# Cross-attention kernel: scores by high parts of both banks first, and x's split ahead of exp and normalise

## The reference

```python
def _layernorm(x, axis=-1, eps=1e-05): ...
x = x + _L0_xattn_ref(ctx_1024, _layernorm(x), fside, fside, ...)   # layernorms with weights, q/k/v, softmax(q k^T), @ Wout
#   q = q * (1.0 + scale) + shift ;  qk = einsum(q, k) * 64**-0.5 ; attn = softmax(qk) ; out = attn @ v @ Wout
x = x + tanh(_layernorm(x) @ weight @ aux_weight1 @ aux_weight2 + bias)
```

## Time and profile before

| | |
|---|---|
| median of 3 runs | 2071.06 us (2065.18 to 2071.54) |
| profiled execution | 2069.4 us |
| its span | 2067.6 us |
| TensorE's mean granted clock | 0.997 |
| busy: PE, DVE, ACT, POOL | 98%, 76%, 66%, 67% of the span |
| DMA packets | 464.11 MB, SyncE's queue 79.2% of 16 engines' span |

### The profile page before, as it was taken

How to read it: one execution, slowest core, us unless ns; L and a number is a source line. 1 busy time by engine, 2 the same in 40 slices (tenths; PEclk the granted TensorE clock), 3 DMA queues, 4 the chain that set the end, 5 groups by cost and what they waited for, 6 DMA issues and landing times.

```text
span 2067.6 us, 31929 instructions
## 1 busy us (share of the span) xinstructions
PE 2017.8 (98%) x9072; PEld 1661.6 (80%) x9072; DVE 1573.8 (76%) x2470; ACT 1364.1 (66%) x3125; POOL 1393.7 (67%) x1529
## 2 busy tenths in 40 slices
PE   8998999999999999999999999999999999999998
PEld 6887878888788788878888788878888788878887
DVE  7567876776677787787777877778777877888776
ACT  4455667666676766776667676666666666666654
POOL 2136767666577777677766777777776777777664
PEclk9999999999999999999999999999999999999999
DMA  7657989989788788978898798888877567866663
GB/s 259 196 176 219 275 233 256 265 241 262 210 249 256 207 236 242 260 217 225 233 260 242 205 234 238 243 229 221 230 228 241 171 204 208 236 197 196 189 171 121
DMA packets 524864, 464.11 MB, mean 224 GB/s; under 512 B 56720, under 2 KB 416272, under 8 KB 524688
## 3 DMA queue, kind: packets, MB, share of 16 engines
q1 hardware_dynamic: 524688, 462.06, 79.2%
HBM read 279.64 MB, written 182.26 MB: 223 GB/s over the span
## 4 chain that ended last, share of the span: by engine, by line
PE 32%; DVE 18%; SPq 15%; ACT 10%; issue 10%; POOL 7%; DMA 4%; DVEq 0%; ACTq 0%; POOLq 0%
PE bank L168 12%; PE bank L1246 8%; PE bank L173 6%; POOL area L1547 5%; PE bank L1251 4%; DVE pT_lo L1430 3%; ACT area L1291 3%; DVE turned L1421 3%; DVE area L1399 2%; ACT pT_hi L1296 2%; DVE row_max L1404 2%; SPq L1127 2%; SPq L726 2%; SPq L1145 2%; SPq L1157 2%
## 5 line engine op out<-in xcount | busy, mean ns | idle before, releaser
L1547 POOL TENSOR_TENSOR area<-area,row_max 128x256 f32<-128x256 f32 x512 | 353.0, 710 | 105.3 <-DVE row_max L1404 100.1
L1296 ACT CAST pT_hi<-turned 128x512 fp32r<-128x512 f32 x256 | 159.3, 622 | 400.8 <-DVE turned L1421 400.7
L168 PE MATMUL bank<-M_hi,xT_hi 128*128 128x512 f32 x1024 | 402.7, 393 | 14.4 <-ACT xT_hi L1080 14.4
L168 PE MATMUL bank<-M_lo,xT_hi 128*128 128x512 f32 x1024 | 401.4, 392 | 0.0
L1571 POOL TENSOR_TENSOR area<-area 128x512 f32<-128x512 f32 x127 | 165.4, 1302 | 269.1 <-ACT area L1337 269.1
L1554 POOL TENSOR_TENSOR area<-area,row_inv 128x512 f32<-128x512 f32 x256 | 269.1, 1051 | 113.7 <-DVE row_inv L1413 113.7
L1410 DVE TENSOR_REDUCE row_sum<-area 128x8 f32<-128x512 f32 x256 | 174.5, 682 | 169.5 <-ACT area L1291 168.6
L1430 DVE TENSOR_TENSOR pT_lo<-turned,pT_hi 128x512 fp32r<-128x512 f32 x256 | 196.6, 768 | 112.3 <-ACT pT_hi L1296 103.7
L173 PE MATMUL bank<-M_hi,xT_lo 128*128 128x512 f32 x1024 | 276.0, 391 | 3.6 <-POOL xT_lo L1085 3.6
L1246 PE MATMUL bank<-N_hi,pT_hi 128*128 128x512 f32 x640 | 249.5, 390 | 3.2 <-ACT pT_hi L1296 1.8
L1246 PE MATMUL bank<-N_lo,pT_hi 128*128 128x512 f32 x640 | 249.6, 390 | 1.5 <-issue 1.4
(11 more groups left out here) (211 smaller groups left out, 4547.9 us busy)
## 6 DMA issues: line engine op xcount, KB each, us to landing
p_scratch<-area SPq DMA_DIRECT2D x256, 256.0 KB, 3.1
p_moved<-p_scratch SPq DMA_DIRECT2D x512, 128.0 KB, 4.2
area<-x_dram SPq DMA_DIRECT2D x128, 256.0 KB, 5.0
area<-x_turned_dram SPq DMA_DIRECT2D x128, 256.0 KB, 4.4
x_scratch<-area SPq DMA_DIRECT2D x127, 256.0 KB, 3.4
x_moved<-x_scratch SPq DMA_DIRECT2D x508, 64.0 KB, 3.5
y_dram<-area SPq DMA_DIRECT2D x127, 256.0 KB, 3.5
land<-m_scratch SPq DMA_DIRECT2D x120, 256.0 KB, 3.2
```

What stands on the lines that cost most here:

```text
L168: mm = eng.matmul(ps, sh, mv, start=(n == 0), stop=False)
L1296: act.copy(half_of(pT_hi, q), turned[:]).then_inc(s_pTh[q], 1)
L1547: last = pool.tensor_tensor(s, s, row.to_broadcast([P, 2, 4, J2]), ALU.subtract)
```

## The change

From tile 3 on the scores are made in another order (`scores_high_first_pe`): for bank 0 and then bank 1 the eight matmuls with `xT_hi`, then for bank 0 and bank 1 the four with `xT_lo`. Each bank's semaphore is raised by its last matmul. ScalarE splits the next tile's x ahead of exp of bank 0 (from slot 3 on), GpSimd ahead of its two `normalise`. In a border slot ScalarE evacuates both banks of the N2 step, and VectorE makes all eight low parts; the second semaphore that GpSimd's part needed is gone. Slots 0 to 2 stay as they were.

```diff
--- before.py
+++ after.py
@@ -603,7 +603,7 @@
         s_n, s_nh, s_nl = sem("s_n"), sem("s_nh"), sem("s_nl")
         s_bin = sem("s_bin")
         s_x2a, s_x2n = sem("s_x2a"), sem("s_x2n")
-        s_last, s_nfree, s_nl_pool = sem("s_last"), sem("s_nfree"), sem("s_nl_pool")
+        s_last, s_nfree = sem("s_last"), sem("s_nfree")
         s_yl, s_bnl, s_rsl = sem("s_yl"), sem("s_bnl"), sem("s_rsl")
         s_kh, s_kl = sem("s_kh"), sem("s_kl")
         s_wo2, s_nev = sem("s_wo2"), sem("s_nev")
@@ -696,9 +696,6 @@
             used, free = free[1], (used, free[0])
         N_of = lambda b: [n_bufs[i] for i in n_at[b]]
         stage_of = lambda b, c: n_raw[:, (n_at[b][1] * PAIRS + c) * D:(n_at[b][1] * PAIRS + c + 1) * D]
-        BY_POOL = (4, 5, 6)
-        BY_DVE = {0: [c for c in range(PAIRS) if c not in BY_POOL], 1: list(range(PAIRS))}
-        lo_before = lambda b: PAIRS * min(b, STACKED) + sum(len(BY_DVE[a % 2]) for a in range(STACKED, b))
         split_at = {TPB * b + c - TPB + 2: (b, c) for b in range(STACKED + 1, B, 2) for c in range(PAIRS)}
         border = lambda t: t % TPB == 1 and t // TPB in range(STACKED, B, 2)
         n2_ps = banks[2:4]
@@ -778,14 +775,7 @@
             for c in cs:
                 eng.wait_ge(s_nh, PAIRS * b + c + 1)
                 hi, lo = (n_cols(y, c) for y in N_of(b))
-                eng.tensor_tensor(lo, stage_of(b, c), hi.bitcast(F32),
-                                  ALU.subtract).then_inc(s_nl if c in BY_DVE[b % 2] else s_nl_pool, 1)
-
-        def n2_made(pe, b, q):
-            of_half = range(4 * q, 4 * q + 4)
-            pe.wait_ge(s_nl, lo_before(b) + sum(c < 4 * q + 4 for c in BY_DVE[b % 2]))
-            if b % 2 == 0 and any(c in BY_POOL for c in of_half):
-                pe.wait_ge(s_nl_pool, len(BY_POOL) * ((b - STACKED) // 2) + sum(c < 4 * q + 4 for c in BY_POOL))
+                eng.tensor_tensor(lo, stage_of(b, c), hi.bitcast(F32), ALU.subtract).then_inc(s_nl, 1)
 
         m_where = lambda c: ((c // 2) % 4, 2 * (c // 8) + c % 2)
         in_pairs = lambda a: a.rearrange("p (i a j) -> p i a j", i=2, j=J2)
@@ -1108,6 +1098,26 @@
             at_least(pe, s_sb[q], t)
             passes(pe, S_ps[q][:], [(st(xT_hi, k), st(xT_lo, k), mo(M_hi_now, k), mo(M_lo_now, k)) for k in range(DC)],
                    (lambda: pe.wait_ge(s_xTl, t + 1)) if q == 0 else None).then_inc(s_sc[q], 1)
+
+        def scores_high_first_pe(pe, t, m):
+            M_hi_now, M_lo_now = M_hi[t // TPB % 2], M_lo[t // TPB % 2]
+            st = lambda y, k: y[:, k * P:(k + 1) * P]
+            mo = lambda y, k, q: y[:, k * INNER + q * BANK:k * INNER + (q + 1) * BANK]
+            pe.wait_ge(s_xTh, t + 1)
+            for q in range(2):
+                if m == 0:
+                    pe.wait_ge(s_ll, t - 4 + 4 * q)
+                elif m == 2 and t < TPB * STACKED:
+                    pe.wait_ge(s_nl, t + 3 + q)
+                pe.wait_ge(s_sb[q], t)
+                for k in range(DC):
+                    for i, mv in enumerate((M_hi_now, M_lo_now)):
+                        pe.matmul(S_ps[q][:], st(xT_hi, k), mo(mv, k, q), start=(k == 0 and i == 0), stop=False)
+            pe.wait_ge(s_xTl, t + 1)
+            for q in range(2):
+                for k in range(DC):
+                    mm = pe.matmul(S_ps[q][:], st(xT_lo, k), mo(M_hi_now, k, q), start=False, stop=(k == DC - 1))
+                mm.then_inc(s_sc[q], 1)
 
         def slot_sp(sp, t, m):
             def store(place, u=t):
@@ -1208,15 +1218,13 @@
                 if (t, place) in tile_at:
                     tile_pe(pe, tile_at[t, place])
 
-            if t < T:
+            if 2 < t < T:
+                scores_high_first_pe(pe, t, m)
+            elif t < T:
                 for q in range(2):
                     if t == 0:
                         pe.wait_ge(s_ml, 8 * q + 8)
                         pe.wait_ge(s_kbo, 15 + q)
-                    elif m == 0:
-                        pe.wait_ge(s_ll, t - 4 + 4 * q)
-                    elif m == 2 and 2 < t < TPB * STACKED:
-                        pe.wait_ge(s_nl, t + 3 + q)
                     scores_pe(pe, t, q)
             if t != 2:
                 tile("A")
@@ -1234,10 +1242,8 @@
                 at_least(pe, s_x2, u)
             for q in range(2):
                 if tile_of(t - 2):
-                    if m == 2 and u < TPB * STACKED:
+                    if m == 2:
                         pe.wait_ge(s_nl, u + 4 + 4 * q)
-                    elif m == 2:
-                        n2_made(pe, u // TPB, q)
                     hi, lo = N_of(u // TPB)
                     ks = range(4 * q, 4 * q + 4)
                     pe.wait_ge(s_pTh[q], u + 1)
@@ -1349,6 +1355,8 @@
                 xT_split_hi(act, t + 1)
             if t > 2:
                 evacuate("A")
+                if t < T - 1:
+                    xT_split_hi(act, t + 1)
             if t < T:
                 exp(0)
             if t < 2:
@@ -1365,12 +1373,13 @@
                 fold_n_act(act, 0, range(5, 6))
                 land_hi(act, 0)
                 fold_n_act(act, 0, range(6, 7))
-            elif t < T - 1:
+            elif t == 2:
                 xT_split_hi(act, t + 1)
-            if t == 2:
                 ln1_stats(act, 3, 3)
             if t in stacked_at:
                 n2_evacuate(act, act.copy, *stacked_at[t], 0)
+                if border(t):
+                    n2_evacuate(act, act.copy, *stacked_at[t], 1)
             evacuate("C")
             if border(t):
                 n2_hi(act, t // TPB, range(0, 4))
@@ -1511,7 +1520,8 @@
                 dve.tensor_tensor(xr[u % RING], O_ps[:], xr[u % RING], ALU.add).then_inc(s_x2, 1)
             sum_tile("C")
             if t in stacked_at:
-                n2_evacuate(dve, dve.tensor_copy, *stacked_at[t], 1)
+                if not border(t):
+                    n2_evacuate(dve, dve.tensor_copy, *stacked_at[t], 1)
             if tile_of(t - 1):
                 if t >= 4:
                     dve.wait_ge(s_x2Tl, t - 3)
@@ -1523,13 +1533,13 @@
                     maximum(0, 2)
                 turn_p(0, t - 1)
                 if border(t):
-                    n2_lo(dve, t // TPB, BY_DVE[0][0:2])
+                    n2_lo(dve, t // TPB, range(0, 2))
                 if t == 1:
                     read_scores(1, 2)
                     maximum(1, 2)
                 pT_lo_part(0, t - 1)
             if border(t):
-                n2_lo(dve, t // TPB, BY_DVE[0][2:])
+                n2_lo(dve, t // TPB, range(2, 8))
             if t in split_at:
                 b, c = split_at[t]
                 n2_lo(dve, b, [c])
@@ -1590,19 +1600,17 @@
             if t == 2:
                 land_lo(pool, 1)
                 xT_split_lo(pool, 3)
+            if 2 < t < T - 1:
+                xT_split_lo(pool, t + 1)
             if t < T:
                 normalise(0)
                 normalise(1)
             if t == 1:
                 land_lo(pool, 0)
-            if 2 < t < T - 1:
-                xT_split_lo(pool, t + 1)
             if 1 < t < T - 1:
                 pow1(pool, t + 1)
             if tile_of(t - 4) and t - 4 < LAST - 1:
                 pow2(t - 4)
-            if border(t):
-                n2_lo(pool, t // TPB, BY_POOL)
             if t == 5:
                 land_lo(pool, t)
 
```

## The result

The changed kernel takes **2082.95 us** (median of 4 runs, 2079.28 to 2084.91) against 2069.57 of the kernel before (four runs, the three of the table ahead among them): a ratio of 1.0069, 95% interval 1.0046 to 1.0091. That is 13.4 us slower. The forecast was 2071, "no difference"; the range (2050 to 2086) holds the result, the sign was missed. The profiled executions differ a little more: the spans are 2067.6 and 2083.1 us, 15.5 apart.

A forecast was written before the change was run, and what follows sets the result against it. TensorE is 98% busy, but a VectorE-to-VectorE loop of 13.77 us, within 0.6 us of TensorE's time, limits gains. Terms 0, +11.1, 0 and -9.2 make +1.9 on 2069.4: 2071 us, range 2050 to 2086.

The forecast's parts named there:

- xT_lo ahead of normalise: Slots 10 to 25: SyncE's second p store goes 0.79 us later per slot; 14 steps make +11.1 us.
- My upper bound, +15: Slots 10 to 25: loss if Wo's store takes 0.3 us more; lower bound 0 if M's store lands earlier.
- Slots 83 to the end: Sum of plain slots -6.5, two borders -2.0 and 14 N2 slots -0.7: -9.2 us.
- Contention: Plain slots: VectorE's pT_lo no longer beside GpSimd's xT_lo, -0.27 us each; 24 behind slot 83 make -6.5.
- The N2 slots: Behind slot 83: 14 slots at the loop's 14.45 us instead of TensorE's 14.50, -0.7.
- The borders: N's low parts and copies redistributed: -2.0 us at the last two borders, about +0.4 each at the four before.
- Slots 26 to 82: Late x about +2 and border +0.4, four times, against 1.9 given back by seven plain slots: 0, bounds -6, +9.
- x comes too late for exp: Rival, chance 0.20: ScalarE's xT_hi waits for its load before exp of bank 0, slots 27 to 81; +9, 2080 us.
- the waits simply go: Rival, chance 0.25: loops have slack, TensorE keeps 14.4 us of xT_hi and six times 0.75 of xT_lo; 2050 us.
- the port only changes hands: Rival, chance 0.13: GpSimd's small power takes xT_lo's place, pT_lo still waits, the 6.5 us aren't given back; 2077 us.
- Slots 4 to 9: Within slots 3 to 9, where TensorE sets the pace: 0.
- Score order: Bank 0 finished 1.8 us later, VectorE waits 0.1 to 0.3 us or keeps phase: cost 0; 0.3 a slot without cover.

The follow-up runs named there:

- the two edits that relieve this loop: Changed kernel with xT_lo behind normalise in slots 10 to 25: 0.9996; changed kernel with SyncE's M store behind the first p store, slots 4 to 25: 0.9957.
- the early store: Changed kernel with SyncE's store of the M tile moved, in slots 4 to 25, from slot's end to right behind the first store of p: 2059.9 us, 0.9957.
- The square above: Four kernels with score order and xT_hi moved; last two borders: neither further part 62.0 us, N part alone 60.4, xT_lo move alone 58.0, both 56.1.

## Why the prediction was wrong

**The step that failed** is the size of "xT_lo ahead of normalise". The mechanism was right in place and kind: the two edits that relieve this loop, each in another way, gave the loss back (0.9996 and 0.9957 from 1.0069). Its sum was +11.1 and is +20.5 (18.3 against the second profile of the kernel before):

- 0.79 us per step for the second store of p was 0.71. But the sum ended there, and the loop ends at the store of the M tile, three issues later. These took 0.5 us more per step: the store of x2 0.96 instead of 0.65, the weights' load 0.79 instead of 0.68, the second p store 0.61 instead of 0.52. Before, SyncE had stood idle for 0.57 us ahead of the second p store; now the six issues stand in an unbroken row. Twelve inner steps, from one evacuation to the next, took 15.09 us on average and take 16.28: 12 x 1.18 = 14.2.
- The first step of each half (at slots 11 and 19) counted like the others in my 14 and lost more: they went from 15.08 to 17.12 and from 15.48 to 17.21, 3.8 together. In the one at slot 11 the second store of p took 1.51 us to issue instead of 0.54, and Wo's in front of it 0.82 instead of 0.64; in the one at slot 19 exp of bank 1 came 0.63 us later behind the evacuation.
- The rest, 2.5, lies at the two folds of N, where TensorE now waits 4.7 us for `N_lo` in two waits; it was 0.87 at each, and in the second profile of the kernel before 0.81 and 2.12. So this part is hardly clear of what varies by itself; the other two are.

My upper bound, +15, took 0.3 us for one later store, and was too narrow for the same reason. The lower bound, 0 if M's store landed earlier, is what the early store showed: with it these slots take 247.1 us.

**Slots 83 to the end** were forecast at -9.2 and gave -9.4 (-9.9, and +0.5 from slot 127 on), but by other terms. Contention went as forecast: `pT_lo` is at 0.69 us everywhere behind slot 83, and the powers didn't take `xT_lo`'s place, as in slot 89 of the changed kernel:

```profile
1502.79 1.30 POOL L1075 TENSOR_TENSOR xT_lo<-area,xT_hi 128x512 fp32r<-128x512 f32 x1
```

```profile
1506.62 0.69 DVE L1439 TENSOR_TENSOR pT_lo<-turned,pT_hi 128x512 fp32r<-128x512 f32 x1 [0.81 <-ACT pT_hi L1302]
```

The loop did get shorter by the 0.27 us, from 13.77 to 13.49, from one read of bank 0 to the next in plain slots of the changed kernel:

```profile
1671.45 0.71 DVE L1408 SCALAR_TENSOR_TENSOR area<-bank,rs,area 128x512 f32<-128x512 f32 x1
...
1684.94 0.71 DVE L1408 SCALAR_TENSOR_TENSOR area<-bank,rs,area 128x512 f32<-128x512 f32 x1
```

Yet the plain slots gave 2.2 us, not 6.5: none took less than TensorE's 13.6, the loop was at 13.77, and where the slot holds an M tile (14.1 before and after) the loop didn't bind at all. I took the gain of the loop without asking where the next bound lies. The N2 slots were at TensorE's 14.51 before and after, so the -0.7 for them was nothing either: a loop shorter than TensorE's slot can't shorten it. Nor are the 2.2 us the contention's alone: the score order by itself gave them too, with `pT_lo` at 779 ns; `xT_hi` ahead of exp took them back, and only then was `xT_lo`'s move needed for them.

The borders gave what was missing: slots 98 and 99 went from 31.6 to 27.3 and 114 and 115 from 32.6 to 28.7, -8.1 together against -2.0. A wait of 1.5 us ahead of the N2 step in slot 106 and 1.2 us less in slot 83 make up the rest. Of TensorE's waits for x at slots 99 and 115, 5.3 us in the kernel before, my sum counted nothing as regained, since the loop was to take it all back; at these borders it did not. The square above says that there the N part is worth the forecast's 2.0 us and `xT_lo` no longer being late some 4. Six low parts took 4.80 us, not 3.8:

```profile
1408.10 4.80 DVE L778 TENSOR_TENSOR Wo_hi<-n_raw,N_lo 128x512 fp32r<-128x512 f32 x6
```

Two errors of 4 to 6 us cancelled, so the term's agreement is luck and no merit of its working.

**Slots 26 to 82**, forecast at 0 (-6 to +9), were +0.2. Against the second profile of before they are +1.9. `xT_hi` does wait for its load, 43.3 us in 45 waits, but exp behind it waits 70.7 us less for GpSimd. The rival "x comes too late for exp" gave 2080, near the measured 2083, by +9 us in slots 26 to 82 that aren't there. The rival "the waits simply go" would have needed slots 10 to 25 unharmed; with them mended, the kernel is at 2059.9, so about half of its 18.9 us was there to be had. (Its six waits for `xT_lo` were 3.6 us in all, not six times 0.75, so the sum should have been 18.0.) The rival "the port only changes hands" fell with `pT_lo` at 0.69.

**Slots 4 to 9**, forecast at 0, took 98.8 us instead of 96.0 (96.1 in the second profile of before). The early store gives back 1.1 of it, not the 2 expected there; the rest was not followed and stays open.

**Score order** was costed at 0; alone it measured +0.28%, and with `xT_hi` +0.39%. Part of that is in the tail and at the borders; the rest is too thin in a single profile to be placed, and stays open.

## What to carry to other kernels

When a step is moved on one engine, follow its loop to the instruction that closes it, through every issue of the queue on the way: here the closing one was a store three issues behind the one that was priced. A gain on one loop counts only down to the next bound (here 2.2 us of 6.5), and a loss that comes from a store behind others in one queue is mended in the queue, by one moved issue, and not by giving up the change. A wait that is due to a chain of two late producers (`xT_hi`, then `xT_lo`) gave nothing here while only the first was moved. And before a sum over a few stretches of one profile is explained, take a second profile of the same kernel: six borders differed by 3.1 us here with nothing changed.

## What was unexpected in the hardware's behaviour

The same DMA issue on SyncE takes a different time in different stretches. The store of x2, 256 KB each time, took 0.65 us to issue at 349.80 in the kernel before, 0.96 at 376.26 in the changed one and 1.94 at 370.20 in the kernel with the early store; the median over slots 10 to 25 is 0.65, 0.91 and 1.14 us in these three. It is tempting to blame the missing pause in the queue ahead of it, but the kernel before shows the same issue slow with a pause of 0.56 us ahead of the store of p in front of it,

```profile
364.15 0.54 SPq L1127 DMA_DIRECT2D p_scratch<-area  x1
364.73 0.99 SPq L1194 DMA_DIRECT2D x_scratch<-area  x1
```

and quick behind four issues (the two of `wo` in one row) with none:

```profile
1782.19 1.34 SPq L1127 DMA_DIRECT2D p_scratch<-area  x1
1783.57 1.11 SPq L736 DMA_DIRECT2D wo<-wo_scratch  x2
1784.73 0.56 SPq L1127 DMA_DIRECT2D p_scratch<-area  x1
1785.33 0.62 SPq L1194 DMA_DIRECT2D x_scratch<-area  x1
```

What sets it was not tried and stays open.

The other thing is where two executions of one kernel differ. In the two profiles of the kernel before, slots 10 to 22 agree to 0.01 us, but for 0.1 in slot 16, and everything from slot 83 on to 0.2 in all; the rest differs in a few slots: slot 25 by +2.9 us (a fold of N), slot 32 by +1.5, slot 66 by -1.5 and slot 82 by -1.7. A difference of 2 us that lies in one such slot says nothing, one that comes in small equal steps over twelve slots does.
